# Second layer's prologue: POOL clears the values, gathered tiles are added singly, the output projection loads earlier

## What is computed

```python
x = x + _L0_xattn_ref(_layernorm(x), ctx_1024, ctx_1024, mask_Bx1x1xS2_ff1, wq, bq, wk, bk, wv, bv, wo, bo)
x = x + _L0_ffn_ref(_layernorm(x), ...)      # 2 shared experts, 2 of 8 routed
x = x + _L1_xattn_ref(_layernorm(x), ctx_1024, ctx_1024, mask_BxS2_bf0, Wq, bq, Wk, bk, Wv, bv, Wo, bo)
x = x + _L1_ffn_ref(_layernorm(x), theta, phi, theta_noise, phi_noise)
# an attention: softmax((q k^T) / sqrt(16) + mask) v, then the output projection wo, bo
```

## Time and profile before

| | before |
|---|---|
| three timed runs, median | 1310.09 us |
| lowest and highest | 1309.3, 1310.26 us |
| the profiled execution, its span | 1309.3 us |
| PE busy | 90% of the span |
| ACT busy | 79% |
| DVE busy | 58% |
| POOL busy | 14% |
| mean granted clock of PE | 0.984 |

### The profile page before, as it was taken

How to read it: one execution, slowest core, us unless ns; L and a number is a source line. 1 busy time by engine, 2 the same in 40 slices (tenths; PEclk the granted TensorE clock), 3 DMA queues, 4 the chain that set the end, 5 groups by cost and what they waited for, 6 DMA issues and landing times. The chain is left out here.

```text
span 1309.3 us, 43655 instructions
## 1 busy us (share of the span) xinstructions
PE 1174.6 (90%) x17942; PEld 581.8 (44%) x17942; DVE 757.7 (58%) x1660; ACT 1038.9 (79%) x1482; POOL 181.0 (14%) x223
## 2 busy tenths in 40 slices
PE   8888898898898999998999999878889999998994
PEld 5322232232222457667999999542223223222222
DVE  5336867767667686445666666654346445444446
ACT  3599999999999853542666666449999999999992
POOL 5111111110020110232000000243220000000000
PEclk9999999999999999999999999889999999999997
DMA  7237734534627151312343343222120000000001
GB/s 194 66 122 235 239 109 153 163 106 159 192 94 253 43 174 45 110 49 83 91 136 110 117 149 113 80 80 76 38 60 11 21 27 2 20 27 3 2 3 64
DMA packets 105952, 124.94 MB, mean 95 GB/s; under 512 B 24963, under 2 KB 88798, under 8 KB 105790
## 3 DMA queue, kind: packets, MB, share of 16 engines
q1 hardware_dynamic: 88368, 85.66, 21.1%
q0 software_dynamic: 9888, 29.76, 7.2%
q10 hardware_dynamic: 7534, 7.16, 1.8%
HBM read 70.27 MB, written 46.95 MB: 90 GB/s over the span
## 5 line engine op out<-in xcount | busy, mean ns | idle before, releaser
L861 ACT ACTIVATE prob<-banks 128x1024 f32<-128x1024 f32 (+1 forms) x832 | 772.6, 1049 | 12.5 <-PE banks L1592 8.9
L1607 PE MATMUL banks<-prob,v 64*32 64x512 f32 x6656 | 442.2, 592 | 0.6 <-ACT prob L861 0.6
L1592 PE MATMUL banks<-zone,kst 52*32 52x512 f16 x6528 | 336.7, 383 | 89.7 <-ACT prob L861 80.9
L1592 PEld LDWEIGHTS banks<-zone,kst 52*32 52x32 f16 x6528 | 92.7, 89 | 498.0 <-ACT prob L861 477.8
L1607 PEld LDWEIGHTS banks<-prob,v 64*32 64x32 f32 x6656 | 118.8, 106 | 21.7 <-ACT prob L861 2.4
L2224 PE MATMUL banks<-xsT_d,w 128*128 128x128 f16 x1776 | 124.7, 220 | 2.9 <-issue 2.9
L2224 PEld LDWEIGHTS banks<-xsT_d,w 128*128 128x128 f16 x1776 | 109.6, 98 | 12.0 <-issue 8.5
L2235 PE MATMUL banks<-w,hh 128*128 128x256 f16 x592 | 107.5, 274 | 0.0
L1110 DVE RECIPROCAL late<-late 128x512 f32<-128x512 f32 x31 | 103.9, 3353 | 1.1
L2031 DVE TENSOR_TENSOR hl<-hid,hh 128x128 f16<-128x128 f32 x296 | 83.2, 291 | 32.2 <-ACT hh L1962 24.6
L1958 ACT ACTIVATE hid<-banks,b 128x128 f32<-128x128 f32 x222 | 74.7, 369 | 26.2 <-PE banks L2224 20.6
(11 more groups left out here) (277 smaller groups left out, 1302.0 us busy)
## 6 DMA issues: line engine op xcount, KB each, us to landing
weight_parts<-late SPq DMA_DIRECT2D x54, 256.0 KB, 3.5
w<-weight_parts POOLq DMA_DIRECT2D x24, 512.0 KB, 3.9
late<-in_L_ffn_W_r SPq DMA_DIRECT2D x43, 256.0 KB, 4.3
weight_parts<-more SPq DMA_DIRECT2D x26, 256.0 KB, 3.5
zone<-q_parts SPq DMA_DIRECT2D x180, 32.0 KB
slot_rows<-late POOLq DMA_DIRECT2D x14, 384.0 KB, 4.5
more<-in_L_ffn_W_r SPq DMA_DIRECT2D x21, 256.0 KB, 4.1
xs_d<-slot_rows ACTq DMA_DIRECT2D x39, 128.0 KB
```

The source lines that it names most:

```text
L861: nc.scalar.activation(prob[0:m, t % P_RING, 2 * (n % 2):2 * (n % 2) + 2, :], score[G % S_RING][0:m, :, :], ACT.Exp, scale=0.25).then_inc( ...
L1592: last = nc.tensor.matmul(score[G % S_RING][j:j + wide, a, :], kst[stack, 2 * q + n % 2, t * P + j:t * P + j + wide], qst[stack, u % Q_RIN ...
L1607: last = nc.tensor.matmul(outp[u % 2][GROUP * j:GROUP * (j + 1), a, :], v[rows, t, u % NQ, j, :], prob[rows, (u * KT + t) % P_RING, j, :], ...
```

## The change

In layer 1 alone, with layer 0's order kept by a branch:

1. `clear_values` runs on POOL behind the eight gathers of chunk 0, no longer on DVE.
2. DVE writes the low key parts before it splits the mask. Each gathered tile of chunk 0 has its own semaphore, and `combine_tile` adds one tile; products of bounds stand between the tiles, the statistics and the turned tokens.
3. On PE the eight bounds come ahead of the queries, each followed by a tile of values; two tiles stand before them, four at the end. The bank ring's order of jobs changes with it.
4. ACT loads the table of exponentials and issues its key loads before the first copy of values. After the queries it issues six of the 12 first query loads, SP the other six.
5. The 17 loads of the output projection are issued by SP in the experts' part, into tiles of their own at a fixed address.
6. POOL's all-reduce stands ahead of the first two gathers of chunk 1.

```diff
-V_FIRST = (0, 9)
-V_MORE = (0, 11)
+V_MORE = (0,)
...
+PROJECTION_AT = 226240
+
+V_BEFORE = 7
+V_BETWEEN = 9
...
-        jobs = keys + queries + bounds
+        jobs = keys + queries + bounds if first else keys + bounds + queries
...
+        def load_first_queries(eng, u, s, heads):
+
+            for jj in heads:
+                a, i = jj % 2, jj // 2
+                eng.dma_start(qst[lanes_of(a, s), u, i, :],
+                              qparts[jj:P:BLOCK_HEADS, 0, Q_STACK[s], :]).then_inc(q_loaded[u], 16)
...
-                load_first_queries(0, s)
+                load_first_queries(sp, 0, s, range(QH if first else 2))
...
-                    gather(pool, home[0], 0, n, gathered[0])
+                    gather(pool, home[0], 0, n, tile_gathered[n // 2])
+                clear_values()
...
-            load_projection()
+            if first:
+                load_projection(nc, pool, w, wo, bo, bvp, wo_loaded, bo_loaded, bv_loaded)
+            pool.wait_ge(sized, 7)
+            nc.gpsimd.partition_all_reduce(widest[:], sizes[:], P, bass.bass_isa.ReduceOp.max).then_inc(widest_ready, 1)
             if not first:
                 for n in range(FIRST_GATHERS):
                     paced_gather(1, n)
-            pool.wait_ge(sized, 7)
-            nc.gpsimd.partition_all_reduce(widest[:], sizes[:], P, bass.bass_isa.ReduceOp.max).then_inc(widest_ready, 1)
...
+            else:
+                for n in range(len(KCH)):
+                    high_part("k", 1, n)
+                act.wait_ge(k_split, len(KCH))
+                load_keys(act, 0, range(2, len(K_STACK)))
+                table_of_exponentials()
+                act.wait_ge(v_cleared, 5)
+                for t in range(V_BEFORE):
+                    values(t)
                 untangle_queries()
...
+                for o in range(DH):
+                    high_part("q", o, 0)
+                act.wait_ge(q_split, 1)
+                for s in range(len(Q_STACK)):
+                    load_first_queries(act, 0, s, range(2, QH))
+                for t in range(V_BETWEEN, KT):
+                    values(t)
...
+            def combine_tile(i):
+
+                dve.wait_ge(tile_gathered[i], 16 * 2)
+                for k in range(2):
+                    n = 2 * i + k
+                    if k:
+                        dve.wait_ge(added, n)
+                    nc.vector.scalar_tensor_tensor(g.x[:, i, :], home[0][:, n, :], g.weight[:, k, i:i + 1], g.x[:, i, :],
+                                                   ALU.mult, ALU.add).then_inc(added, 1)
...
-            if not first:
-                for b in range(2):
-                    nc.vector.memset(beside(b), 1.0).then_inc(v_cleared, 1)
...
+            def later_preparations():
+                for n in range(len(KCH)):
+                    low_part("k", 0, n)
+                mask_parts()
+                for n in range(len(KCH)):
+                    low_part("k", 1, n)
+                bound_matrix()
+                combine_tile(0)
+                split_weights()
+                combine_tile(1)
+                combine_tile(2)
+                for n in range(2):
+                    bound_product(0, n)
+                combine_tile(3)
+                query_statistics(0)
+                for n in range(2, len(BCH)):
+                    bound_product(0, n)
+                normalise(0)
+                largest(0)
+                for n in range(2):
+                    bound_product(1, n)
+                low_turned()
+                for n in range(2, len(BCH)):
+                    bound_product(1, n)
+                for name in queries:
+                    low_part(*name)
+                largest(1)
...
+            def later_products():
+                half = len(BCH)
+                for t in range(2):
+                    project_values(t)
+                pe.wait_ge(a_ready, 1)
+                pe.wait_ge(high_ready, high["k", DH - 1, len(KCH) - 1] + 1)
+                for n in range(half):
+                    bound(0, n)
+                    if n:
+                        norm(n - 1)
+                    project_values(2 + n)
+                bound(1, 0)
+                norm(half - 1)
+                project_values(half + 2)
+                turn_x()
+                for n in range(1, half - 1):
+                    project_values(V_BEFORE + n - 1)
+                    bound(1, n)
+                    norm(half + n - 1)
+                bound(1, half - 1)
+                pe.wait_ge(untangled, DH)
+                pe.wait_ge(wq_split, 1)
+                for o in range(DH):
+                    project_queries(o)
+                for n in range(half - 2, half):
+                    norm(half + n)
+                for t in range(V_BETWEEN, KT):
+                    project_values(t)
...
+            load_projection(nc, sp, l1, g.wo, g.bo, g.bvp, g.wo_loaded, g.bo_loaded, g.bv_loaded)
+
             sp.wait_ge(routed, 1)
```

More of the change, by code:

```diff
@@ L266, in attention @@
         else:
-            gathered = [sem(f"gathered{c}") for c in range(NC)]
+            gathered = [None] + [sem(f"gathered{c}") for c in range(1, NC)]
+            tile_gathered = [sem(f"tile_gathered{i}") for i in range(TPC)]
             added, power_ready, rooted, final_done, out_stored = (
@@ L970, in _ @@
             dve.wait_ge(sized, 1)
-            if not first:
-                for b in range(2):
-                    nc.vector.memset(beside(b), 1.0).then_inc(v_cleared, 1)
-                dve.wait_ge(v_cleared, 2)
-                nc.vector.memset(v[HALF:P, KT - 1], 0.0).then_inc(v_cleared, 1)
-                dve.wait_ge(v_cleared, 3)
-                for b in range(2):
-                    nc.vector.memset(beside(b)[HALF:KLAST, KT - 1:KT], 1.0).then_inc(v_cleared, 1)
             if first:
@@ L1523, in project_values @@
                 last.then_inc(v_projected, 1)
-            bound_matrix()
-            if not first:
-                for t in range(V_FIRST[layer]):
-                    project_values(t)
-                turn_x()
-                for t in range(V_FIRST[layer], V_MORE[layer]):
-                    project_values(t)
-            pe.wait_ge(untangled, NCT + DH)
-            pe.wait_ge(wq_split, 1)
-            for o in range(DH):
-                project_queries(o)
-            pe.wait_ge(a_ready, 1)
@@ L1537, in _, with first_products @@
-            pe.wait_ge(high_ready, high["k", DH - 1, len(KCH) - 1] + 1)
-            if first:
+            def first_products():
+                pe.wait_ge(untangled, NCT + DH)
+                pe.wait_ge(wq_split, 1)
+                for o in range(DH):
+                    project_queries(o)
+                pe.wait_ge(a_ready, 1)
+                pe.wait_ge(high_ready, high["k", DH - 1, len(KCH) - 1] + 1)
                 pe.wait_ge(heads_ready, 3)
                 pe.wait_ge(wv_loaded, 16)
-            rest = range(V_MORE[layer], KT - V_LATE)
@@ L1542, in _ @@
-            for i, (_, o, n) in enumerate(bounds):
-                bound(o, n)
-                if i:
-                    norm(i - 1)
-                for t in rest[i * len(rest) // len(bounds):(i + 1) * len(rest) // len(bounds)]:
-                    project_values(t)
-            norm(len(bounds) - 1)
-            for t in range(KT - V_LATE, KT):
-                project_values(t)
+                rest = range(V_MORE[layer], KT - V_LATE)
+                for i, (_, o, n) in enumerate(bounds):
+                    bound(o, n)
+                    if i:
+                        norm(i - 1)
+                    for t in rest[i * len(rest) // len(bounds):(i + 1) * len(rest) // len(bounds)]:
+                        project_values(t)
@@ L1552, in _ @@
+            bound_matrix()
+            if first:
+                first_products()
+            else:
+                later_products()
             with safe_is_off(pe):
```

125 lines of the change are left out of this document (67 added, 58 removed).

## The result

The changed kernel takes 1300.95 us in the median of four runs (1300.07 to 1302.77), the kernel before 1310.17 beside it (1309.3 to 1311.52): a ratio of 0.9937, 95% interval 0.9925 to 0.995, 9.2 us less. The direction and the place are as forecast, the gain is half as large again.

What follows compares the result with a forecast made beforehand. The time to the first exponential in layer 1's 47 us prologue was taken as the bound: 8.5 us earlier, less the clock's price, gains 6.1, so 1310.09 - 6.1 = 1304.0 us, range 1301.3 to 1307.3.

Steps and rivals of the forecast that it cites:

- The chain: Layer 1's prologue, from POOL's clears through values, bounds, adds, queries and ACT's issues: first exponential 8.5 us earlier.
- The clock: PE's granted clock falling to 1.2 GHz in two waits of the prologue: gain cut from 8.5 to 6.1 us.
- the first wait: PE idle from 845 or 847 to 848.7 us, before the third values tile: clock fall costs 1.2 us.
- the second, ahead of tiles 11 and 12: PE idle from about 866 to 868.3 us: clock fall priced at 1.2 of a possible 1.9 us.
- The branch: PE's step just ahead of the first scores: 0.74 us, as in the old trace.
- B: POOL's clears hold DVE's adds beside them: 2.6 us more, 1306.6 us; chance 0.12.
- C: Query load issues on ACT and SP take turns: 3.3 us more, 1307.3 us; chance 0.08.
- D: First exponential earlier, but a later unit waits for chunk 1's rows or keys: about 1309 us; chance 0.06.
- E: POOL's clears behind eight gathers become the chain; slower, 1313 us, if they take 12.7 us; chance 0.04.
- The table of exponentials and the key loads on ACT: Placed ahead of the values, in ACT's wait from 842 to 848.3 us: cost nothing.
- The projection loads on SP: 17 issues, 11 us, in the experts' part behind 489.62, SP's next work at 542.71: cost nothing.
- The span: Traced 1309.3 us against timed runs of 1309.3 to 1310.26: nothing worth a term lies around it.

Runs made afterwards that it cites:

- again_after: The changed kernel run and traced once more, unedited: 1299.68 us, ratio 0.9935 to the kernel before.
- before_projection_reduce: Kernel before with only the projection loads on SP and the all-reduce ahead of the first gathers of chunk 1: 1308.80 us, ratio 1.0004.
- clears_split_2: Changed kernel with the two large clears on DVE between low key parts, small ones left on POOL, second run: 1297.14 us, ratio 0.9907.
- pool_as_before: Changed kernel with the 17 projection loads and two gathers of chunk 1 back on POOL ahead of the all-reduce: 1305.64 us, ratio 0.9977.
- queries_sp: Changed kernel with all 12 first query loads issued by SP, as before the change: 1303.65 us, ratio 0.9969.
- clears_twice: Changed kernel with POOL's two large clears made twice behind the gathers: 1303.48 us, ratio 0.9967.
- changed_3: The changed kernel run and traced a third time, unedited: 1299.98 us, ratio 0.9933 to the kernel before.
- again_before: The kernel before, run and traced once more, unedited: one timed run, 1306.98 us.

## Why the prediction was right, and where its size was off

**The chain.** It stands step by step. Against the layer's begin, with the clock kept up, the sum had the clears' end at 15.4, the second product at 17.6, the normalised rows at 23.0, the turn at 23.8, the low parts at 27.8, the low query at 30.6, the issues' end at 35.0, tiles 11 and 12 at 37.3 and the first exponential at 38.6. In again_after they are 15.2, 17.8, 23.3, 24.0, 28.0, 31.1, 34.9, 37.5 and 38.25. The sum of 8.5 us before the clock comes out near what was measured: the mean prologue of three traces of either code (before_projection_reduce counted with the kernel before) is 47.35 and 38.77, 8.6 apart. That is in part luck: in this difference the 0.5 us of the branch, which the sum left out, and the 0.5 that the clock cost in the mean cancel.

**The clock is the mis-sized term.** 2.4 us were taken off. For the first wait I took 1.2 as a certainty; it was 1.36, 0.2 and 0 in three executions. For the second, ahead of tiles 11 and 12, I took 1.2 of 1.9; after 2.34 to 2.36 us of wait these tiles took 1.99 in all three. It is not impossible: in clears_split_2 they took 2.44 behind such a wait. A term that comes in some executions and not in others belongs in the range, with its mean in the sum; 0.5 instead of 2.4 would have given 1302.1, and with the branch below 1301.6. What remains to 1300.95 is within the scatter between medians: the three groups with the changed kernel give 9.2, 7.9 and 8.9 us. One reading behind the term was off: a mean of 0.59 from 838 to 840 says that the clock fell near the begin of that stretch, at about 838.4, not at its end.

**The branch.** 0.74 was carried over from before; 0.27 is there now, 0.5 us that the sum did not take, since the flags are set at 872.0, 3.5 us ahead of the scores. In the three traces in which the flags come last (the kernel before's two and pool_as_before) the scores start 1.1 us after them; where the flags lie 1.3 us or more ahead and no load is late, PE's gap is 0 to 0.33.

**Rivals.** B: the adds beside the clears take 0.48 to 0.50 us, not held. The Trainium skill, "SBUF — State Buffer", section "Who interferes with whom", has it so for a DVE instruction with two SBUF inputs beside a POOL instruction that only writes; the trace agrees. C: queries_sp and the two rows of issues refute it: each queue keeps its 0.61 to 0.63 us per issue of 16x512 while the other issues. The Trainium skill, "Perfetto Trace Analysis", section "DMA Instruction — HWDGE (DVE, Sync)", has one generator that two sequencers share and lock; no such lock shows in these issues. D: chunk 1's normalised rows end at 910.66 and PE turns them at 916.14; of 11.2 us of slack 5.7 went, "some 6 go at most". E: that the clears start the chain is real (clears_twice), but they take 4.0 us, as in layer 0, and not 12.7.

**Costed at nothing.** The table of exponentials and the key loads on ACT lie in its wait for the clears, as forecast: nothing. The projection loads on SP end far ahead of SP's next work, as forecast, but PE's wait for an expert's weights at 762 us, 1.05 in the mean against 0.1, came with them in ten of eleven traces. How loads that were issued 260 us earlier could do that was not settled: in changed_3 the four weight loads, each issued when the one before has landed, take 13.6 us from the first to the last issue, in again_before 12.6, and the traces don't tell why. The price, a tenth of the gain, is measured; its cause stays open.

**The span.** Of the span it was said that nothing worth a term lies around it. In the profiled executions whose own time is known, 1.7 to 2.0 us do (1301.18 against 1299.4; 1306.98 against 1305.0). It cancels in the difference, but with it the first trace of the kernel before stands for some 1311 us (an estimate), one of its longer executions, which is what the 4.6 us of waits in its units show too.

## What to carry to other kernels

Undo each part in the finished version as well as making it alone: where two chains end together (here PE's last tiles and POOL's reduce), a part is worth nothing alone and some six microseconds with the others. When an operation moves to another queue, list what stands behind it there; put ahead, the clears held up the gathers and the mask on POOL or the keys on DVE; put between the low key parts, where DVE was waiting anyway, they were nearly free. Ahead of comparing two traces stage by stage, trace one kernel twice: stages that the change doesn't touch moved by 1 to 5 us here. And set each trace against the timed runs: the one of pool_as_before was the slowest of ten and tells 8 us where the medians tell 6.

## What the runs showed of the hardware

The granted clock falls or stays behind the same 3.25 us of waiting, in the same code, from execution to execution (six microseconds at 0.52, three at 0.51, none). Behind 5.8 to 7.2 us it was at its lower level when PE resumed, in all six traces that have such a wait; behind 4.54 us it fell some 0.8 us after PE had resumed. A wait of 2.0 us in the experts' part took the clock in nine of fourteen traces, at about 1.6 us each. POOL stood idle for 5.79, 6.23 and 6.94 us between a gather and the all-reduce, with nothing to wait for in the record; where the root stood between them and POOL waited 11 us or more, the all-reduce followed its semaphore by 0.14 us. In queries_sp the last query load of 16x512 landed 2.0 us after its issue had ended.
